# Counting neighbour ranks in quarters of 256 columns, with VectorE carrying the counts, in a graph layer kernel

## What is computed

```python
adj_ = jnp.where(eye, 1.0, adj)
neigh = (adj_ > 0) & ~eye
ni = neigh.astype(jnp.int32)
rank = jnp.cumsum(ni, axis=-1) - ni        # neighbours before this one in the row
nb = ni.sum(-1)
skip = jnp.maximum(jnp.where(nb > T, (nb + K - 1) // K, 1), 1)    # T, K = 10, 2
rem = neigh & (sk > 1) & (rank % sk == sk - 1) & mask[:, :, None]
rem = rem | jnp.swapaxes(rem, 1, 2)
```

## Time and profile before

| | |
|---|---|
| median of 3 runs | 1401.79 us (1400.84 to 1404.13) |
| the profiled execution, its own time | 1393.88 us |
| its span in the profile | 1392.0 us |
| TensorE busy | 1196.3 us, 86% |
| VectorE busy | 1128.0 us, 81% |
| ScalarE busy | 934.8 us, 67% |
| GpSimd busy | 708.3 us, 51% |
| mean granted TensorE clock | 0.92 |

### The profile page before, as it was taken

One profiled execution on the slowest core, in us unless ns is written; L12 is line 12 of the kernel. 1 busy time (PEld: TensorE's weight loads), 2 busy tenths in 40 slices (PEclk: granted clock), 3 DMA queues, 4 the chain that ended last, 5 costly groups with the idle time before them and its releaser, 6 DMA issues. The chain is left out here.

```text
span 1392.0 us, 32405 instructions
## 1 busy us (share of the span) xinstructions
PE 1196.3 (86%) x12833; PEld 882.8 (63%) x12833; DVE 1128.0 (81%) x2092; ACT 934.8 (67%) x1691; POOL 708.3 (51%) x988
## 2 busy tenths in 40 slices
PE   4879999999898999889979989899899988687451
PEld 4758676867676776567757657667667766464320
DVE  3442499998998889888998979999899999989950
ACT  1787788786778687767758768686767878533310
POOL 0463354454268645765365744685357554704025
PEclk9988999999999999899998999999999999998655
DMA  4446454645144443435244432436144321420000
GB/s 138 133 153 195 142 163 123 199 136 185 49 155 156 148 127 110 139 112 181 96 140 129 128 108 100 156 127 211 33 157 160 122 86 36 149 64 32 1 8 15
DMA packets 119033, 167.09 MB, mean 120 GB/s; under 512 B 58816, under 2 KB 59472, under 8 KB 118864
## 3 DMA queue, kind: packets, MB, share of 16 engines
q1 hardware_dynamic: 103168, 117.72, 28.6%
q0 software_dynamic: 14336, 46.42, 8.7%
q10 hardware_dynamic: 1360, 0.74, 0.2%
HBM read 114.25 MB, written 50.59 MB: 118 GB/s over the span
## 5 line engine op out<-in xcount | busy, mean ns | idle before, releaser
L535 PE MATMUL psL<-H0A,AT 128*128 128x65 f32 x2048 | 261.5, 287 | 17.1 <-issue 9.7
L535 PEld LDWEIGHTS psL<-H0A,AT 128*128 128x128 f32 x2048 | 252.5, 203 | 27.1 <-issue 23.3
L1471 POOL DMA_INDIRECT rows<-VR,IDX x128 | 173.5, 1356 | 81.4 <-ACT JUNK L851 51.9
L1241 DVE TENSOR_TENSOR HUB<-HUB 128x1472 f32<-128x1472 f32 (+6 forms) x224 | 182.1, 813 | 9.0 <-ACT HUB L953 6.3
L1242 DVE TENSOR_TENSOR HUB<-HUB 128x1472 f32<-128x1472 f32 (+6 forms) x224 | 187.9, 839 | 0.0
L546 PE MATMUL psT<-UM,NEIT 128*128 128x512 f16 (+3 forms) x1024 | 164.7, 312 | 25.4 <-ACT VR L819 12.8
L638 PE MATMUL psG<-OHB,HL 128*64 128x384 f16 (+5 forms) x2048 | 172.9, 319 | 10.8 <-DVE OHB L1176 8.3
L845 ACT ACTIVATE VR<-psT 128x512 f16<-128x512 f32 x256 | 147.3, 598 | 50.9 <-PE psT L574 42.8
L1512 POOL DMA_INDIRECT out<-FR x128 | 149.4, 1167 | 37.5 <-issue 36.5
L629 PE MATMUL psG<-OHB,HL 128*64 128x256 f16 (+1 forms) x2560 | 154.6, 280 | 0.1
L953 ACT ACTIVATE HUB<-HUB 128x1472 f32<-128x1472 f32 (+5 forms) x168 | 90.5, 539 | 88.5 <-DVE HUB L1242 86.4
(11 more groups left out here) (134 smaller groups left out, 2218.3 us busy)
## 6 DMA issues: line engine op xcount, KB each, us to landing
AT<-in_adjt SPq DMA_DIRECT2D x128, 512.0 KB, 4.6
RR<-rows SPq DMA_DIRECT2D x128, 288.0 KB
FR<-rows SPq DMA_DIRECT2D x16, 272.0 KB, 4.9
X<-in_x SPq DMA_DIRECT2D x16, 256.0 KB, 3.6
h<-VR SPq DMA_DIRECT2D x16, 256.0 KB, 4.7
rows<-VR,IDX POOLq DMA_INDIRECT x128, 4.4
out<-FR POOLq DMA_INDIRECT x128
CH<-in_ch ACTq DMA_DIRECT2D x1, 192.0 KB, 4.3
```

The costliest lines, as they stand in the source:

```text
L535: m = e.matmul(ps["L"][:, 65 * t:65 * t + 65], AT[:, n % RING, kk, t * P:t * P + P], H0A[:, T * b + 2 * kp + kk, :], start=(kp == kk == t ...
L1241: e.tensor_tensor(b0, a0, a1, ALU.max)
L1471: e.indirect_dma_start(row_d[:, :], bass.IndirectOffsetOnAxis(ap=IDX[:, gb % 2, t:t + 1], axis=0), VR[:, t, :].bitcast(I32), None).then_in ...
```

## The change

A tile's 1024 columns are counted in four quarters (q) of 256 in place of two chunks of 512. A bank now holds one quarter of two neighbouring tiles. It takes four products as before, now of 256, 128, 256 and 128 columns. ScalarE empties it in two instructions of 256 columns, one for each tile, since each has its own bias. A half has eight banks as before and three carries in place of one. The carry moves from GpSimd to VectorE, with the semaphore v_car in place of o_car. A quarter's count waits for the marks of its own 256 columns, not for those of all, and the next graph's marks wait only for the counts of their own quarter. The two halves of a graph have strands of their own, D and C, and the list of steps is another one throughout.

```diff
+QCOLS = 256
 ORDER = (
-    "XnnnUUUAAAMMWUUMMARUADDMADUUDAADWMDDDDTUMDDDDDAUMBDDDDURMUMBBMNBrrTANBBABBAMrNUUgUrWrrrrhsscksssAAAl"
...
+    "XnnUUnAAWMMUMUUDDAAMRDUUADDMDDDCDDDMAAUCAWCCCCCCCCMUUCTTBBBBBBBMBRrrAAWMUUNrrrrMMMrrNNAUUssgAUcssssc"
...
-            for t in range(4 * hf, 4 * hf + 4):
-                add("D", "cum", g, b, t, 0)
-            add("D", "car", g, b, hf)
-            for t in range(4 * hf, 4 * hf + 4):
-                add("D", "cum", g, b, t, 1)
+            for q in range(4):
+                for t in (4 * hf, 4 * hf + 2):
+                    add("DC"[hf], "cum", g, b, t, q)
+                if q < 3:
+                    add("DC"[hf], "car", g, b, hf, q)
...
-            def ranks_up(g, b, t, ch):
-                w.wait_ge(o_diag, 2 * (2 * g + b) + t // 4 + 1)
-                w.wait_ge(v_nei, nth["nei", g, b, t // 4, 3] + 1)
-                o = t_free("cum", g, b, t, ch)
-                for kk in range(4):
-                    at = COLS * (4 * ch + kk) + P * (t % 4)
-                    m = e.matmul(o[:, kk * P:COLS], half(t // 4)[:, at:at + P], UM[:, 0:COLS - kk * P],
-                                 start=(kk == 0), stop=(kk == 3), skip_group_check=True)
+            def ranks_up(g, b, t, q):
+                hf = t // 4
+                if q in (2 * hf, 2 * hf + 1):
+                    w.wait_ge(o_diag, 2 * (2 * g + b) + hf + 1)
+                w.wait_ge(v_nei, nth["nei", g, b, hf, q] + 1)
+                o = t_free("cum", g, b, t, q)
+                for i in range(2):
+                    for kk in range(2):
+                        at = COLS * (2 * q + kk) + P * (t % 4 + i)
+                        m = e.matmul(o[:, QCOLS * i + P * kk:QCOLS * i + QCOLS], half(hf)[:, at:at + P], UM[:, 0:QCOLS - kk * P],
+                                     start=(i == kk == 0), stop=(i == kk == 1), skip_group_check=True)
                 m.then_inc(t_full, 1)
...
-            def ranked(g, b, t, ch):
-                u = t_use("cum", g, b, t, ch)
+            def ranked(g, b, t, q):
+                u = t_use("cum", g, b, t, q)
                 w.wait_ge(t_full, u + 1)
-                if ch:
-                    w.wait_ge(o_car, nth["car", g, b, t // 4] + 1)
-                elif 2 * g + b:
-                    w.wait_ge(d_sca[t], 16 * (2 * g + b))
-                bias = CB[:, t:t + 1] if ch else CF[:, CF_UNMARK:CF_UNMARK + 1]
-                e.activation(VR[:, t, COLS * ch:COLS * ch + COLS], t_bank(u), ACT.Identity, bias=bias).then_inc(t_empty, 1)
+                if q:
+                    w.wait_ge(v_car, nth["car", g, b, t // 4, q - 1] + 1)
+                for i in range(2):
+                    if q == 0 and 2 * g + b:
+                        w.wait_ge(d_sca[t + i], 16 * (2 * g + b))
+                    bias = CB[:, t + i:t + i + 1] if q else CF[:, CF_UNMARK:CF_UNMARK + 1]
+                    m = e.activation(VR[:, t + i, QCOLS * q:QCOLS * q + QCOLS], t_bank(u)[:, QCOLS * i:QCOLS * i + QCOLS],
+                                     ACT.Identity, bias=bias)
+                m.then_inc(t_empty, 1)
...
-                    w.wait_ge(t_full, t_use("cum", gb // 2, gb % 2, 4 * hf + 3, 1) + 1)
+                    w.wait_ge(t_full, t_use("cum", gb // 2, gb % 2, 4 * hf + 2, kp) + 1)
...
+            def carry(g, b, hf, q):
+                tiles = slice(4 * hf, 4 * hf + 4)
+                before, cb = VR[:, tiles, QCOLS * (q + 1) - 1], CB[:, tiles]
+                w.wait_ge(t_empty, t_use("cum", g, b, 4 * hf + 2, q) + 1)
+                e.tensor_scalar(cb, before, 0.75, -UNMARK, ALU.is_gt, ALU.mult).then_inc(v_in, own.up())
+                w.wait_ge(v_in, own.n)
+                e.tensor_tensor(cb, cb, before, ALU.add).then_inc(v_car, 1)
...
-            def carry(g, b, hf):
-                tiles = slice(4 * hf, 4 * hf + 4)
-                before, cb = VR[:, tiles, COLS - 1], CB[:, tiles]
-                w.wait_ge(t_empty, t_use("cum", g, b, 4 * hf + 3, 0) + 1)
-                e.tensor_scalar(cb, before, 0.75, -UNMARK, ALU.is_gt, ALU.mult).then_inc(o_in, own.up())
-                w.wait_ge(o_in, own.n)
-                e.tensor_tensor(cb, cb, before, ALU.add).then_inc(o_car, 1)
```

More of the change, by code:

```diff
@@ new lines @@
+    "ksscssSScssscScSsAAAsscSRcMMMUSSSDDhADDDDMWRClLDDDCDDXCCCNNCCNTCCCCBnBnnTUgUAAMUMWBMABBrBBBrrrrrrrsU"
+    "UsshAAskMccsscssUcUSSSSRMAAssslUssccsssccDDMMASSDDDDSFDSMUCCCCCDLFFWDCCUCCDDLLRCCUFFFNNNMMLLFAFFTTBB"
+    "BBAMBBBddmmrLUALUBedFmdmFeArrdFdMrrmAgrmhrrsssskseUddclcsssmmcAcddssSSsemmUddseWSSccmSRLKKKffsmdSKsK"
+    "LssdDDcMDFDDmmDKVVcUDDddSDeSeDAAMKKMUCMRUCCCCmDAFFtAmWNvCCCddTvCCCeLLmFFNmeBUBTFddNmmXBLLBBBABBnFFdd"
+    "FrrrrrrergmmrnddssntsteLLsssccWMkUssMoUtsssssAccctGSSSSKMMKQRtsstAsmMDDcmFQccUUUtDDDMMFFAAtQMSSDDSDG"
@@ new lines @@
+    "QSALQCLCddtCtmWCCCRUFmtFFCCCLLhDDDtCTMQQAFFFQQCTtUQQUgBBLLFQelFFMtrMBBAABBBBUddrmmrrrNMdrrrUUekessNt"
+    "NssssLLhssssccccsssSSSSQQJJJJJmtQQddmQAAQttsFFFaffRmdmtQLedccedtttttttUmmLttMcQQSddQSsAesWcAUDSMMADD"
+    "DDQSQMQQCVVlmFCFmDRFXDdNdDQQCCWNDCLLQQDDQTNCCCenCvmCQUUCUdnmmQBTBBBBBBBnFFFdAAdMQrrrrrrrUMgmQQrQMQAd"
+    "ssssssssEKKskMeKKmKKccecUcmssddeUEEcssvSSWmSSSsmsRcDDoddmeAsAKKADtLLccDDKUKmMSddQEEAEeFSFEEDDDSFtMDD"
+    "DEEtULLACCtFMUUTBBmmeCCCMFEFtQdAAWdGmRGmCCCddrCQtCCmmQQheTtrteLLFUFFMMMBBBglBBQBLLNrrArFFFaLQLQrrrUQ"
@@ new lines @@
+    "NtNksstssssFFFUQsssstsUcccsAAcsQcsAcJJWhddmmMQtdmJJdtSSSSSSeRssQdmLLtMlccdJtmmddCeeSQFFFmmtDQQtdtUUD"
+    "AttSAtDDtdLMCMMUUtDttLOOtDtmmDDCCFFtQdCUQRDWDDQtNeQQQFXCQQCQeNQCdNffmQQnQQCCCQAnQmTnTQQQABrMBBBBBBBL"
+    "LdgVQFFdrrrrMrrrMWQkQssKsVsssssKKKvEsFccmemddKKcKKsccsvmUmddLLsUsSSSSseseSADDDMsoAmmAEEDDddeUmFRFmMK"
+    "ectddAFEUDDDMQKcctAMSUtLLAEEStmCSCmdFUtUCEeCCEdWmFFAEDtLLEECCCMDDmQQtCCCFFFddTLQQmLtRteTmFFFgUQQLBMt"
+    "LAFFFBeQQtrBdhrMMQQdlBBULUBBABMrLmrUQNrdtmFFFrrrWemdssssssssNAJAtJJJJOkscscstcQNcmsdQedhsccmmeQQtSdd"
@@ new lines @@
+    "SSSDmmSSRDlddtDMUUOstDDmmQtttcQGssdtcdetMDMmtttQttttQQMQAeQQLLDADSQQGSCQDDQCRQaDFAXQQNCCQdNQFFmffQQN"
+    "UTUCmdQWmCVVBBQQCCCCCEEEenrvLLEETKnEKnBFFddEeErmBBmEBgUddrBFBGErErrrmAtmevrModdkssssssssAssMMULLAUcc"
+    "cScSSSKcKKKKKFFUKmAmeKMeFddWssssDDLLssRcMQFFmcctAFDDtDmQtdUGMAUDdDDASSSAtCSCCLMCCtWQCMDDDLQQUUCCORte"
+    "mmFFFQLQCCCtLddetaMFFFLLmQQTTmtgBBQQAUAehlBBBMQMJBArBrrBrrJrrrkFFFsstssssULLNsssJJJsssssddtAmUtmNccc"
+    "OdNMdtQQcetFmmSSSSUUssccddmmRFFtQcMSQeddSAhWUfftMMAtQQettcAtttDDmmttMAttWLSStDDDtQdDDUDUQQQmdQQLFQlQ"
@@ L63 @@
+    "sssssQQtdtccQQtcQQLLtccFSQQSSStSSSdFSFmQtemdtdtGQeQLmmethJJJLJJFFFtLLFFFQtLLtQQQttOltFFFQtddtmmtddmm"
+    "tdtedtmmdLLQQdteemmQdQQFFFdQQLLmaQdmQffQeeFFFdQQLKQLQmmKKQQdQmdQdVVQvmdFFFEKeKeKmmvddemmGGddeLLFFFLL"
+    "mmKKetKtEdtEodtEEmKtEmEEEtdeQdttFFFQQmtmQQtddmQQtmeQQteQQtJtJJtQJtJttQQtQQttQQtttttQOtttQQQQQQQQQQQa"
+    "EEQQQQQQQQEEEEOEEEEEEEOO"
 )
@@ L406, in program @@
         a_bat = sem("a_bat")
+        v_car = sem("v_car")
         (v_pad, v_mkf, v_mk, v_h0, v_h1, v_l, v_rem, v_lo, v_any, v_oh, v_wm, v_red, v_wz,
@@ L416, in program @@
         v_mean, cen_made = sem("v_mean"), (sem("v_cen"), sem("o_cen"))
-        o_diag, o_car, o_thin, o_cls, o_idx, o_x1, o_flag, o_coef, o_fin, o_nv, o_zero, o_in = (
-            sem(n) for n in ("o_diag", "o_car", "o_thin", "o_cls", "o_idx", "o_x1", "o_flag", "o_coef", "o_fin", "o_nv", "o_zero", "o_in"))
+        o_diag, o_thin, o_cls, o_idx, o_x1, o_flag, o_coef, o_fin, o_nv, o_zero, o_in = (
+            sem(n) for n in ("o_diag", "o_thin", "o_cls", "o_idx", "o_x1", "o_flag", "o_coef", "o_fin", "o_nv", "o_zero", "o_in"))
         f_d, f_p, f_l = sem("f_d"), sem("f_p"), sem("f_l")
@@ L1347, in vector @@
                     low_parts(*a)
+                elif kind == "car":
+                    carry(*a)
                 elif kind == "res":
@@ L1399, in thin @@
                 last = VR[:, tiles, N - 1]
-                w.wait_ge(t_empty, t_use("cum", g, b, 4 * half + 3, 1) + 1)
+                w.wait_ge(t_empty, t_use("cum", g, b, 4 * half + 2, 3) + 1)
                 w.wait_ge(v_mk, 1)
@@ L1518, in gpsimd @@
                     no_loops(*a)
-                elif kind == "car":
-                    carry(*a)
                 elif kind == "thin":
```

43 lines of the change are left out of this document (10 added, 33 removed).

## The result

The changed kernel took 1420.9 us in the median of 12 runs (1406.9 to 1425.4), the kernel before 1400.7 us beside it: a ratio of 1.0131 (1.0107 to 1.0155), 20.2 us. The forecast of 1395 us had the wrong sign: 7 us less were forecast. The profiled execution of the changed kernel took 1409.2 us (span 1407.4), 15.4 us of span over the one read before. It is one of the two shortest of the twelve, and its granted TensorE clock, 0.913, is high: the twelve have 0.906 in the mean. Its rows account for the 15.4 us, not for all of the 20.2.

A forecast was written before the change was run, and what follows sets the result against it. TensorE and VectorE were both taken as close to full from 150 to 1140 us, neither bounding alone. Start -4, carries +30, their waits +12, vanished waits -42, GpSimd -3: -7 us, so 1395 us (1372 to 1422; forecast's own 1380 to 1399).

The forecast's parts named there:

- I take two thirds of the 49 and a third of the 28 [...]: -42 us: Middle stage: TensorE's saving removes part of VectorE's 49 us of waits on TensorE and 28 on ScalarE, -42 us.
- below 20: Sign of being right: VectorE's waits on TensorE in the preparations' stage fall below 20 us, from 49.
- a microsecond taken from TensorE and one put on VectorE weigh about the same: Premise from the chain that ended last, where VectorE has 13% and TensorE 12% of the span.
- which its idle time hides except where TensorE needs the bank: ScalarE's wait for VectorE's 96 carries: could be 40 us, mostly hidden by ScalarE's idle time.
- carries +30 predicted: Middle stage, VectorE: 78 carries at 0.38 us each add 30 us (27 to 31).
- their waits +12 predicted: Middle stage: VectorE waits 0.16 us before each of 78 carries for ScalarE, +12 us (0 to 94).
- GpSimd's -3: GpSimd's queue, rid of the carry, shortens TensorE's 12.3 us of waiting for the diagonal: -3 us (0 to -12).
- -4 was put: Start, 100 to 150 us: 16 groups of products, each 0.231 us shorter, give their saving in full, -4 us.
- VectorE pays at the carry: Rival: waits at the head of VectorE's queue cost 0.5 us a carry, 39 us in all; 1422 us, chance 0.24.
- TensorE was the bound: Rival: all 49 us of VectorE's waits on TensorE and half of those on ScalarE go; 1366 us, chance 0.13.
- The clock takes it back: Rival: less busy TensorE gets a clock 0.037 lower, losing 32 of 48 us saved; 1423 us, chance 0.08.
- TensorE waits for banks instead: Rival: ScalarE empties banks slower (0.70 us) than TensorE counts (0.41), so TensorE waits; 1423 us, chance 0.05.

The follow-up runs named there:

- e8_columns_padded: The changed kernel with each bank's first product issued three times, restoring 1280 columns a group: 1.0186 times the kernel before.
- e2_columns_only: The kernel before, old list and moves, with only the fewer product columns (768 a group); some counts left out: 1.0004 times the kernel before.
- e3_moves_split: The kernel before with each 512-column ScalarE move split into two of 256: 1.0034 times the kernel before.
- e9_no_carry: The changed kernel, new list, with no carry on any engine; counts of earlier quarters left out: 0.9857 times the kernel before.
- e10_carry_unawaited: The changed kernel with VectorE's 96 carries and their waits, but ScalarE awaiting none; earlier quarters' counts left out: 0.9975 times the kernel before.
- e18_unawaited_beside: The changed kernel with carries made but not awaited by ScalarE, run again beside the changed kernel (1.0082): 0.9953 times the kernel before.
- e7_chunks_new_list: The kernel before (chunks of 512, one move a bank, carry on GpSimd) in the new list of steps: 1.0183 times the kernel before.
- e4_carry_vectore: The kernel before, old list, with its 32 carries on VectorE in place of GpSimd: 1.0118 times the kernel before.
- e6_quarters_old_list: The changed kernel's code (quarters, two moves a bank, carries on VectorE) in the old list of steps: 1.0756 times the kernel before.
- batches D and E: Two batches of follow-up runs, kernel before at 1440.7 and 1444.6 us; the unaltered changed kernel had ratios 1.0036 and 1.0082 there.
- e5: The changed kernel again, unaltered, beside other runs on the same chip: 1.0120 times the kernel before.

## Why the prediction was wrong

**The step that failed first** is "I take two thirds of the 49 and a third of the 28 [...]: -42 us". Its size was too large, and its reason was wrong. In the middle stage VectorE's idle time falls from 101.9 to 86.5 us; less the 9.8 at the carry it is 76.7, so 25.2 us went and not 42. The waits on TensorE fell by 28 us, from 49.1 to 21.4 (33 were taken, and "below 20" was the sign); those on ScalarE, apart from the carry, stayed at 28 (9 were taken). But the fall does not come from the saved columns. With the columns back in e8_columns_padded the waits are still 24.7 us, and with the columns alone in e2_columns_only VectorE's waits on TensorE over the whole execution are 108.0 us, 109.7 in e3_moves_split beside it. It comes in good part from the carries: e9_no_carry has 41.1 us of these waits and e10_carry_unawaited 20.8. VectorE's added work stands where it waited before. The sum charged the carries in full and also credited the waits that they take the place of to TensorE's saving, and of that saving the runs show 0 to 9 us: nothing by e2_columns_only, 9 of 50 us by e8_columns_padded.

The premise behind it, that "a microsecond taken from TensorE and one put on VectorE weigh about the same", was read off the chain that ended last. By the runs one on TensorE weighs 0.2 us (e8_columns_padded), and VectorE's 45 us of carries with their 37 us of waits weigh 17 us.

**The step that was left out** is ScalarE's wait for a carry, "which its idle time hides except where TensorE needs the bank". The wait was sized well, 33.5 us against "could be 40", and no term was put for it. It is not hidden: e18_unawaited_beside is 19 us faster without it by the ratios, 14 by the medians. TensorE's need of the bank is a part of it, since its waits for a bank that a rank move must empty fall from 29.4 to 16.6 us with it. Whether that is all is open, as TensorE waits 20 us longer for VectorE there. That the delay is also handed on through the rest of a half's chain (the following quarters, the thinning on GpSimd, the distances on ScalarE) is my reading and was not tested.

**The ledger of VectorE up to the last rank product.** It starts at 1156.5 us, before at 1132.5: 24.0 later. From 150 us to there VectorE is busy for 917.1 us, before for 883.4, and idle for 89.4, before for 99.1. The terms: carries +30 predicted, +37.5 measured; their waits +12 predicted, 12.5 measured; other idle time -45 predicted (with GpSimd's -3), -22.2 measured; other work -3.8. The measured ones sum to +24.0. In the first 150 us VectorE is busy for 7.0 us more, 7.5 of carries, so nothing is gained there where -4 was put. What follows the last rank product took 250.9 us instead of 259.5; 24.0 - 8.6 = 15.4 us is the difference of the spans. The -8.6 was in no step.

**Sizes.** A group of rank products got 0.182 us shorter (46.5 / 256), not 0.231. TensorE as a whole shed only 21.7 us: its other products took 24.8 us more, 1056.4 in place of 1031.6. The old form in the new list (e7_chunks_new_list) has 1047.4 at nearly the old clock, so some 16 of these go with the list and the rest with the clock. A carry costs 0.47 us and not 0.38. A move costs 202.65 / 512 = 0.396 us, inside the bounds but near the upper one, 203 us in all. TensorE's 12.3 us of waiting for the diagonal are gone, as the -3 assumed.

**The rivals.** "VectorE pays at the carry" gave 1422 us, close to the result, but by luck: it took a wait of 0.5 us a carry, and measured are 9.8 / 75 = 0.13 in the middle stage, near the value of the forecast. Its mechanism is seen in e4_carry_vectore and e6_quarters_old_list, where the list gives no cover, and not in the changed kernel. "TensorE was the bound" is out by e2_columns_only. "The clock takes it back" is right in part. In the middle stage the clock is 0.95, 0.96 before, above the 0.90 named as its sign; but over all executions beside each other it is 0.907 in place of 0.921, and it comes back to 0.916 with the columns. Its price was 0.037 of clock and 32 of 48 us; the runs show 0.01 and some 11 of 50. "TensorE waits for banks instead" is not out either. Before rank products alone these waits fell from 11.4 us to 8.4 in the middle stage, but before all products of the ring they rose from 12.7 to 19.4, and in the whole execution from 14.1 to 29.5. Its other half, that little of VectorE's waits vanishes by the saving, is what e8_columns_padded shows. It had been given a chance of 0.05.

**What the runs add up to**, in ratios: without any carry the quarters gain 1.4%, 21 us where -49 was the prediction's sum for all gains. VectorE's side of the carries costs 17 us where 42 was put, and ScalarE's 19 us (14 by medians) where nothing was put. That leaves 10 to 15 us of loss; 17 and 20 us were measured where the kernel before takes 1400 us, and 5 and 12 in batches D and E (11 and 12 by medians). The parts come from different batches, and why the loss is less there is open.

## What to carry to other kernels

When work is cut into smaller pieces that hand a result from one to the next, price the chain between the engines and not only the instructions: here 96 hand-overs, of 0.50 us each where nothing else is in hand, cost 31 to 36 us, and 47 us of saved matrix products brought 0 to 9. A hand-over must be charged on both engines that wait. Waits on an engine that is 93% busy do not show what a saving there is worth: they can go because the waiting engine got more work. Padding the saved work back in measures the worth with one line, and the granted clocks of the two should be compared as well. Judge a changed form and its order of steps separately: the same code was 7.6% slower in the old order and 1.2% in the new.

## What the runs showed of the hardware

**Small VectorE instructions stretched by GpSimd.** The carry's sum L1148 has a median of 0.166 us and a mean of 0.266; 13 of 96 take over 0.5. The timeline of the changed kernel shows with what they coincide:
```profile
579.67 0.15 DVE L1146 TENSOR_SCALAR CB<-VR 128x4 f32<-128x4 f16 x1
579.83 1.26 POOL L1515 TENSOR_TENSOR FR<-FR,HID 128x512 f32<-128x512 f32 x1 [2.37 <-DVE HID L1290]
579.86 1.25 DVE L1148 TENSOR_TENSOR CB<-CB,VR 128x4 f32<-128x4 f32 x1
...
581.21 1.20 ACT L826 ACTIVATE VR<-psT,CB 128x256 f16<-128x256 f32 x3 [2.64 <-DVE CB L1148]
```
An addition of four columns lasts as long as GpSimd's of 512 that began 0.03 us earlier, to 0.01 us. ScalarE's idle time of 2.64 us ends with it, and 1.1 of them are the stretching. The same pairs stand at 206.3 us (1.04 and 1.04), 656.5 (1.03 and 1.04) and 1056.7 (1.15 and 1.15), and all 13 end within 0.03 us of the end of a GpSimd TENSOR_TENSOR that began first. Over the medians the stretching is 45.4 - 96 x 0.329 = 13.8 us, most of it in L1148. The rows from which the carry was priced have one input each or read the accumulation banks; L1148 has two inputs in SBUF. The Trainium skill has the rule (SBUF — State Buffer, section "SBUF: two separate sides"): the port pair that VectorE and GpSimd share is locked for a whole instruction, by a VectorE operation with two SBUF inputs against a GpSimd one that reads SBUF, and the loser waits. The trace agrees. Four instances of L1146, which has one input, are also over 0.5 us, and three of them end within 0.03 us of the end of such a GpSimd instruction as well. The rule as told covers inputs in pairs only, so for these the trace shows the coincidence and no cause:
```profile
1066.88 1.27 POOL L1515 TENSOR_TENSOR FR<-FR,HID 128x512 f32<-128x512 f32 x1
1067.20 0.98 DVE L1146 TENSOR_SCALAR CB<-VR 128x4 f32<-128x4 f16 x1
```

**Two levels of time.** The kernel before takes 1399 to 1401 us in two batches and 1441 to 1454 in four, with chip numbers 2 and 8. In the slower batches the traces hold stretches in which three engines stand nearly idle together, here in e3_moves_split (busy times as in group 1):
```profile
797.00:815.00 18.00, 6.31 (x34) 2.24 (x34) 3.62 (x6) 5.32 (x11) 12.04 (x13) 0.64 0.28 106
```
GpSimd issues one indirect DMA after another in it, and the waits that end in the stretch are ended by "remote" (13.08 us on VectorE) and "issue". VectorE has no wait ended by "remote" in any of the six traces of the faster batches, before, after and e5 to e8. That these engines lack instructions there is a guess; nothing was run on it.
